# Negative parts, second norms and the masked key sums of a two-layer transformer block on one core

## The chip, the core and the metric

The kernel runs on one core of a Trainium2 chip. A core has a matrix engine (TensorE, "PE" in the profile, with its weight loads as "PEld"), three engines for everything else (VectorE "DVE", ScalarE "ACT", GpSimd "POOL"), and a queue that issues transfers ("SP"). Each runs its own instructions in program order and waits for the others on semaphores. The metric is device time in microseconds (us): the median of several runs.

## What is computed

Two transformer layers on 2 x 1024 rows of 256 numbers in float32. Only the parts that the change touches are shown in full: the norm, and the linear attention of the first layer with its elu.

```python
def _layernorm(x, axis=-1, eps=1e-05):
    m = jnp.mean(x, axis=axis, keepdims=True)
    v = jnp.var(x, axis=axis, keepdims=True)
    return (x - m) / jnp.sqrt(v + eps)

# layer 0 attention (16 heads of 16), on the normalised x
q = _heads(x @ q_w.T + q_b); k = _heads(x @ k_w.T + k_b); v = _heads(x @ v_w.T + v_b)
qp = jax.nn.elu(q) + 1.0
kp = jax.nn.elu(k) + 1.0
kv = jnp.einsum('bhsd,bhse->bhde', kp, v)
z = jnp.einsum('bhsd,bhd->bhs', qp, kp.sum(axis=2))[..., None]
attn = jnp.einsum('bhsd,bhde->bhse', qp, kv) / (z + EPS)
out = attn.transpose(0, 2, 1, 3).reshape(b, s, HID) @ o_w.T + o_b

# the whole
x = L0_attn_hidden_states                     # (2, 1024, 256), float32
xn = _layernorm(x)
x = x + _L0_attn_ref(xn, ...) + _L0_ffn_ref(xn, ...)   # ternary-weight SwiGLU, 256 -> 1024 -> 256
xn = _layernorm(x)
x = x + _L1_attn_ref(xn, ...) + _L1_ffn_ref(xn, ...)   # rotary softmax attention; SwiGLU with Hadamard transforms
return x
```

The kernel writes `elu(z) + 1` as `exp(min(z, 0)) + max(z, 0)`.

## The kernel before

**Tiling.** The 2048 rows are 16 tiles of 128 (`tt`), 4 chunks of 512 (`c`), and two halves (`b`) of 1024. One Python function, `work_order`, writes one list of pieces by hand, and every engine walks through this same list, taking the pieces that it has a part in. So the order on each engine is that of the list, and a piece that waits holds up all that its engine has behind it.

**First layer.** `main(0)` (the feed-forward: `gate`, `up`, `down` for 8 slices of each chunk) is woven with `side0` (the linear attention, then preparations of the second layer's weights) after a start-up of 12 side pieces. For a tile of keys, `kv_in` is: TensorE's product; VectorE adds the bias to keys `zk` (L1194) and to values `ve` (L1195); GpSimd takes `ek = min(zk, 0)` (L1565); ScalarE takes its exp (L1415); VectorE, in `kv_sum`, forms `max(zk, 0) + ek` (L1218). `kv_out` adds the product of keys and values up over 8 tiles in PSUM bank 2; a column of ones in `ve` gives the sum of the keys as a 129th column. After 8 tiles `kv_sums` multiplies by a block mask (a head sees its own 16 rows only): per 128 channels one multiplication by MASK (L1203) and one of eight mask columns by the key sum (L1204). `att_n` multiplies the queries by the result `kvb` (L840) and VectorE divides (L1224 to L1230).

For queries, `q0` is: VectorE takes `min(q + bias, 0)` (L1212) and `max(q + bias, 0)` (L1213) from PSUM, ScalarE the exp (L1419), GpSimd the sum (L1571).

**Norms.** `ln_stats` (VectorE statistics, a power on GpSimd, L1543), `ln_norm` (VectorE: four tiles `(x - mean) * rstd`, L1126, 128 x 256 each), `ln_turn` (TensorE transposes, L789; ScalarE copies the high part XH, L1401; VectorE the low part XL, L1132). Norms 0 to 3 are the first layer's, in the first 40 us; norms 4 to 7 are the second layer's and stand inside the woven list. GpSimd's `bias` (L1552) adds to X after the norm has read it.

The list around the points that matter, in its own order:

- first half's end: `kv_in 7`, `kv_sum 6`, `tern_cut`, `q0 1 0`, `bias 0`, `tern_abs 2` (ScalarE, L1410), `q0 1 1`, `kv_sum 7`, `kv_out 5, 6, 7`, `kv_sums 0`, `att_n 0`
- norm 4: `up 3`, `ln_norm 4`, `bias`, `gate 3`, `att_n 14`, `up 3`, `down 0`, `ln_turn 4`, `att_b`
- norm 5: `up 5`, `down 2`, `ln_norm 5`, `att_b`, `gate 6`, `prep_attn1` (ScalarE, 2.1 us of copies), `up 6`, `prep_down 0`, `down 3`, `ln_turn 5`, `gate 7`, `prep_down 1`

In a layer-0 slice ScalarE takes the tanh of the gate (`gate`, L1459) and a rounded copy of the product (`up`, L1467), VectorE the two products (L1250, L1259), GpSimd the remainder (L1604).

## Time and profile before

| | us |
|---|---|
| median of 3 runs (756.82 to 758.1) | 757.27 |
| the profiled execution's own time | 757.94 |
| its span, first to last instruction | 756.1 |
| busy: PE / DVE / ACT / POOL | 702.5 / 550.8 / 419.2 / 309.3 |
| PE busy, 0 to 80 us / 80 to 260 us | 53.1 / 164.9 |

A row of the timeline gives the start in us from the span's start, the duration, the engine, the line of the kernel, the operation and what it writes and reads; in brackets stand the idle time of the engine before it and what ended that. "x4" is four such instructions in a row, with the duration of all. Busy time of PE is not PE at its peak: the same matmul takes longer at the lower clock.

### The profile page before, as it was taken

To read this page: it belongs to the slowest core of one execution; us is meant where nothing else is said; L and a number is where in the kernel's file an instruction comes from. 1 tells how busy PE (TensorE), PEld (TensorE's weight loads), DVE (VectorE), ACT (ScalarE), POOL (GpSimd) and SP (SyncE) were. 2 spreads that over 40 slices of the span, in tenths; PEclk is the share of its full clock that TensorE was granted. 3 is DMA by queue.
4 is the path that set the end of the run, shared out by engine and by line. 5 is a ranking of instruction groups with operands and counts; after the bars stand their busy time and mean duration, and the time that the engine had idled before them with its cause. 6 is when DMAs were issued, how large, how long until landed. Compare 5 with 4: busy or idle time off the path is not lost.

```text
span 756.1 us, 10955 instructions
## 1 busy us (share of the span) xinstructions
PE 702.5 (93%) x4186; PEld 440.5 (58%) x4186; DVE 550.8 (73%) x896; ACT 419.2 (55%) x560; POOL 309.3 (41%) x285
## 2 busy tenths in 40 slices
PE   4778898979988989999999998999999999999998
PEld 3556797968666778777667675333333333333445
DVE  4896766676677846677888887888888188888415
ACT  2242223424534533343232435999999899999883
POOL 1248766344845856244343541121233213422510
PEclk9898999998999999999999998999999999999999
DMA  6127101001104372251301110344434244432221
GB/s 254 56 84 264 56 2 56 1 1 57 55 1 148 119 262 84 84 196 57 103 11 57 56 57 18 130 145 134 145 89 156 92 164 153 137 110 90 89 92 56
DMA packets 25847, 74.13 MB, mean 98 GB/s; under 512 B 4620, under 2 KB 5996, under 8 KB 24964
## 3 DMA queue, kind: packets, MB, share of 16 engines
q1 hardware_dynamic: 21268, 65.37, 25.9%
q0 software_dynamic: 3808, 7.60, 3.4%
q8 instruction: 33, 0.54, 0.3%
q10 hardware_dynamic: 720, 0.48, 0.2%
q14 instruction: 18, 0.15, 0.1%
HBM read 54.54 MB, written 23.06 MB: 103 GB/s over the span
## 4 chain that ended last, share of the span: by engine, by line
PE 60%; POOL 2%; DVE 2%; ACT 1%; issue 1%; DMA 0%; SPq 0%; DVEq 0%; POOLq 0%; ACTq 0%
PE PS L1020 17%; PE PS L758 12%; PE PS L1006 12%; PE PS L764 8%; PE PS L989 6%; PE PS L979 4%; DVE mx L1321 1%; POOL sg L1613 1%; ACT P L1505 1%; POOL rot L1633 1%; POOL rot L1634 1%; DMA scr_k<-spl 0%; PE PS L995 0%; POOL hl L1604 0%; ACT spl L1487 0%
## 5 line engine op out<-in xcount | busy, mean ns | idle before, releaser
L1505 ACT ACTIVATE P<-PS 128x1024 f32<-128x1024 f32 x256 | 249.4, 1025 | 31.6 <-PE PS L1006 31.2
L1328 DVE TENSOR_REDUCE mx<-PS 128x1 f32<-128x512 f32 x300 | 189.2, 683 | 34.5 <-PE PS L989 32.8
L1321 DVE TENSOR_REDUCE mx<-PS 128x2 f32<-128x1024 f32 x106 | 124.8, 1221 | 37.3 <-PE PS L979 37.0
L1020 PE MATMUL PS<-P,VV 128*32 128x512 f32 x1024 | 137.4, 608 | 0.1
L1604 POOL TENSOR_TENSOR hl<-sg,hh 128x512 fp32r<-128x512 f32 x64 | 84.4, 1319 | 120.0 <-ACT hh L1475 67.4
L1006 PEld LDWEIGHTS PS<-QS,KS 64*128 64x128 f32 x512 | 49.0, 185 | 124.0 <-ACT P L1505 110.8
L1006 PE MATMUL PS<-QS,KS 64*128 64x512 f32 x512 | 117.7, 459 | 2.2 <-DVE mx L1321 1.8
L989 PE MATMUL PS<-KM,QM 64*128 64x512 f32 x300 | 82.3, 402 | 0.0
L1461 ACT ACTIVATE sg<-PS,cols 128x512 f32<-128x512 f32 x32 | 22.1, 690 | 81.9 <-PE PS L758 81.9
L1613 POOL TENSOR_TENSOR sg<-sg,us 128x512 f32<-128x512 f32 x32 | 42.1, 1315 | 37.4 <-ACT us L1470 37.4
L758 PE MATMUL PS<-XH,UGH 128*128 128x512 f32 x128 | 54.1, 422 | 1.6 <-ACT sg L1461 0.8
L758 PE MATMUL PS<-XL,UGH 128*128 128x512 f32 x128 | 50.5, 394 | 0.0
L758 PE MATMUL PS<-XH,UGL 128*128 128x512 f32 x128 | 50.0, 390 | 0.0
L1467 ACT ACTIVATE hh<-sg 128x512 fp32r<-128x512 f32 x32 | 20.2, 632 | 53.5 <-DVE sg L1259 53.5
L1020 PEld LDWEIGHTS PS<-P,VV 128*32 128x32 f32 x1024 | 20.3, 108 | 40.1 <-issue 34.5
L989 PEld LDWEIGHTS PS<-KM,QM 64*128 64x128 f32 x300 | 38.8, 188 | 3.8 <-DVE mx L1328 0.7
L979 PE MATMUL PS<-KM,QM 64*128 64x512 f32 x212 | 39.9, 448 | 0.8 <-DVE mx L1321 0.6
L1459 ACT ACTIVATE sg<-PS,s 128x512 f32<-128x512 f32 x32 | 21.9, 684 | 32.2 <-PE PS L758 32.0
L764 PE MATMUL PS<-DH,hh 128*128 128x256 f32 x128 | 38.0, 297 | 0.0
L1250 DVE SCALAR_TENSOR_TENSOR sg<-sg,PS 128x512 f32<-128x512 f32 x32 | 21.9, 683 | 20.3 <-ACT sg L1459 20.2
L1470 ACT ACTIVATE us<-PS,cols 128x512 f32<-128x512 f32 x32 | 22.0, 688 | 25.5 <-PE PS L758 25.5
L764 PE MATMUL PS<-DL,hh 128*128 128x256 f32 x128 | 36.1, 282 | 0.0
(208 smaller groups left out, 1406.2 us busy)
## 6 DMA issues: line engine op xcount, KB each, us to landing
QM<-scr_q SPq DMA_DIRECT2D x16, 512.0 KB, 4.3
KM<-scr_k SPq DMA_DIRECT2D x16, 512.0 KB, 5.2
QS<-scr_q SPq DMA_DIRECT2D x16, 512.0 KB, 4.4
KS<-scr_k SPq DMA_DIRECT2D x16, 512.0 KB, 5.2
scr_q<-spl SPq DMA_DIRECT2D x24, 256.0 KB, 3.4
scr_k<-spl SPq DMA_DIRECT2D x24, 256.0 KB, 3.5
scr_o<-OE POOLq DMA_DIRECT2D x14, 256.0 KB, 2.7
stg<-in_tern SPq DMA_DIRECT2D x3, 1024.0 KB, 4.8
```

What stands on the lines that cost most here:

```text
L758: i = e.matmul(out, l, r, start=start and j == 0, stop=stop and j == len(pairs) - 1)
L764: i = e.matmul(out[:, r * 256:r * 256 + 256], l, x, start=first and r == 0 and j == 0, stop=last and j == len(pairs) - 1, skip_group_check ...
L979: e.matmul(bank[b + h], QM[p % 2][hr, qt * 128:(qt + 1) * 128], KM[p % 2][hr, chunk(half)], start=True, stop=True).then_inc(q["mt"], 1)
L989: e.matmul(bank[b], QM[p % 2][hr, qt * 128:(qt + 1) * 128], KM[p % 2][hr, chunk(half)], start=True, stop=True).then_inc(q["mt"], 1)
L1006: i = e.matmul(bank[b + h], KS[p % 2][hr, kt * 128:(kt + 1) * 128], QS[p % 2][hr, chunk(half)], start=True, stop=True)
L1020: i = e.matmul(PS[32 * c:32 * c + 32, 7, :], v_head(8 * b + kt, 2 * j + c // 2), P[s % 4][:, chunk(c // 2 + 2 * (c % 2))], start=(kt == 0) ...
L1321: e.tensor_reduce(mx[p % 2][:, :, qt, half], PS[:, b:b + 2, :], AX.X, ALU.max).then_inc(q["mx"], 2)
L1328: e.tensor_reduce(mx[p % 2][:, h, qt, half:half + 1], bank[b], AX.X, ALU.max).then_inc(q["mx"], 1)
L1461: e.activation(s[:, :], bank[b], ACT.Silu, scale=col("wsg", m)).then_inc(q["t"], 1)
L1505: e.activation(P[s % 4][:, half * 1024:(half + 1) * 1024], PS[:, b:b + 2, :].rearrange("p b n -> p (b n)"), ACT.Exp).then_inc(q["ex"], 1)
L1604: e.tensor_tensor(hl[f % 4][:, :], sg[f % 3][:, :], r32(hh[f % 4][:, :]), ALU.subtract).then_inc(q["hl"], 1)
L1613: e.tensor_tensor(s[:, :], s[:, :], us[f % 4][:, :], ALU.mult).then_inc(q["h"], 1)
```

## The change

- **Keys.** GpSimd's minimum (L1565) goes. ScalarE takes `ek = relu(-zk)` itself, then `exp(-ek)` as before in its place in the list.
- **Queries.** VectorE's minimum (L1212) goes. ScalarE takes `relu(-(q) - bias)` from PSUM (with a negated bias column made once), then `exp(-...)`. VectorE's maximum (L1213) now waits until ScalarE's relu has read the bank.
- **Norms 4 to 7.** VectorE only forms `-mean * rstd` (128 x 4, new tile `nmr`); ScalarE does the four tiles as `Identity(x * rstd + nmr)`. The waits for the buffers go with them.
- **Key sums.** `ve` has eight columns of ones instead of one, so the product has 136 columns instead of 129 per 128 channels; MASK is widened by its own eight columns; `kv_sums` is one multiplication of 128 x 272 instead of four instructions.

```diff
 SEMAPHORES = """
-init lns lnv lnd lnr lnn lnb lnh lnl bx fold w0h w0l sus
+init lns lnv lnd lnm lnr lnn lnb lnh lnl bx fold w0h w0l sus
 ta ts tc tl tp tt suh sgd
-kvp kvz kvv kvm kve kvk kvo kvs
+kvp kvz kvv kvm kve kvk kvo kvs mask
 qp qn qr qe qg
...
         IDN = sb("IDN", 25.5, [128, 128])
-        MASK = sb("MASK", 26, [128, 128])
+        MASK = sb("MASK", 26, [128, 136])
         ONES = sb("ONES", 27, [128, 128])
...
         mxc = [sb(f"mxc{i}", 27.8125 + i / 16, [128, 16]) for i in range(2)]
+        MINUS_QB = sb("MINUS_QB", 27.96875, [128, 2])
         MINUS_HALF = sb("MINUS_HALF", 27.9375, [128, 4])
...
         ek = [sb(f"ek{i}", 128 + i, [128, 256]) for i in range(4)]
-        ve = [sb(f"ve{i}", 132 + 1.25 * i, [128, 2, 129]) for i in range(4)]
-        kvb = [sb(f"kvb{i}", 137 + i * 0.5625, [128, 136]) for i in range(2)]
+        ve = [sb(f"ve{i}", 132 + 1.25 * i, [128, 2, 136]) for i in range(4)]
+        kvb = sb("kvb", 137, [128, 2, 136])
         zs = [sb(f"zs{i}", 139 + 2 * i, [128, 512]) for i in range(2)]
...
         mv = [sb(f"mv{i}", 207.5 + i / 32, [128, 4, 2]) for i in range(2)]
+        nmr = [sb(f"nmr{i}", 207.625 + i / 32, [128, 4]) for i in range(2)]
         rstd = [sb(f"rstd{i}", 207.5625 + i / 32, [128, 4]) for i in range(2)]
...
                 for g in range(2):
-                    o = e.matmul(bank[2][:, g * 129:(g + 1) * 129], zk[j][:, g * 128:(g + 1) * 128], ve[j][:, g, :],
+                    o = e.matmul(bank[2][:, g * 136:(g + 1) * 136], zk[j][:, g * 128:(g + 1) * 128], ve[j][:, g, :],
                                  start=(i == 0 and g == 0), stop=(i == 7), skip_group_check=True)
...
                 for g in range(2):
-                    i = e.matmul(bank[b][:, g * 136:(g + 1) * 136], QP[:, g, ts], kvb[g][:, :], start=True, stop=True)
+                    i = e.matmul(bank[b][:, g * 136:(g + 1) * 136], QP[:, g, ts], kvb[:, g, :], start=True, stop=True)
                 i.then_inc(q["an"], 1)
...
                 for i in range(4):
-                    e.memset(ve[i][:, :, 128:129], 1.0).then_inc(q["init"], 1)
+                    e.memset(ve[i][:, :, 128:136], 1.0).then_inc(q["init"], 1)
                 e.memset(MINUS_HALF[:, :], -0.5).then_inc(q["init"], 1)
...
                 e.wait_ge(q["lnr"], n + 1)
-                if n == 6:
-                    e.wait_ge(q["pu"], 4)
-                if n == 7:
-                    e.wait_ge(q["lnb"], 14)
+                if n >= 4:
+                    e.scalar_tensor_tensor(nmr[i][:, :], mv[i][:, :, 0], -1.0, rstd[i][:, :], ALU.mult, ALU.mult).then_inc(q["lnm"], 1)
+                    return
                 for t in range(4):
...
                 e.tensor_scalar(s16b[:, :], cols[:, z:z + 8], 1.0 / 32, None, ALU.mult).then_inc(q["sus"], 1)
+                e.tensor_scalar(MINUS_QB[:, :], cols[:, COLS["qb0"][0]:COLS["qb0"][0] + 2], -1.0, None, ALU.mult).then_inc(q["sus"], 1)
+                e.wait_ge(d["c"], 48)
+                e.tensor_scalar(MASK[:, 128:136], MASK[:, 0:128:16], 0.0, None, ALU.add).then_inc(q["mask"], 1)
...
                     e.wait_ge(q["an"], 8)
-                for g in range(2):
-                    e.tensor_tensor(kvb[g][:, 0:128], bank[2][:, g * 129:g * 129 + 128], MASK[:, :], ALU.mult)
-                    i = e.tensor_scalar(kvb[g][:, 128:136], MASK[:, 0:128:16], bank[2][:, g * 129 + 128:g * 129 + 129], None, ALU.mult)
-                i.then_inc(q["kvs"], 1)
+                e.wait_ge(q["mask"], 1)
+                e.tensor_tensor(kvb[:, :, :], bank[2][:, 0:272].rearrange("p (g n) -> p g n", g=2),
+                                MASK[:, :].rearrange("p (o n) -> p o n", o=1).broadcast_to([128, 2, 136]), ALU.mult).then_inc(q["kvs"], 1)
...
                 i = 2 * c + m
-                e.wait_ge(q["qp"], i + 1)
-                if i >= 2:
-                    e.wait_ge(q["qg"], i - 1)
-                e.tensor_scalar(zs[m][:, :], bank[b], col("qb0", m), 0.0, ALU.add, ALU.min).then_inc(q["qn"], 1)
+                e.wait_ge(q["qn"], i + 1)
                 e.tensor_scalar(QP[:, m, chunk(c)], bank[b], col("qb0", m), 0.0, ALU.add, ALU.max).then_inc(q["qr"], 1)
...
                 e.dma_start(IDN[:, :], ident_d).then_inc(d["idn"], 16)
-                for t, src in ((MASK, mask_d), (HAD, had_d), (BKV, bkv_d)):
+                for t, src in ((MASK[:, 0:128], mask_d), (HAD[:, :], had_d), (BKV[:, :], bkv_d)):
                     e.dma_start(t[:, :], src).then_inc(d["c"], 16)
+
+            def ln_norm(n):
+                c, i = n % 4, n % 2
+                if n < 4:
+                    return
+                e.wait_ge(q["lnm"], n - 3)
+                if n == 6:
+                    e.wait_ge(q["pu"], 4)
+                if n == 7:
+                    e.wait_ge(q["lnb"], 14)
+                for t in range(4):
+                    e.activation(ln_buffer(n)[:, t, :], X[:, 4 * c + t, :], ACT.Identity, bias=nmr[i][:, t:t + 1], scale=rstd[i][:, t:t + 1]).then_inc(q["lnn"], 1)
...
             def kv_in(tt, b):
+
                 j = tt % 4
+                e.wait_ge(q["kvz"], tt + 1)
+                if tt >= 4:
+                    e.wait_ge(q["kvk"], tt - 3)
+                e.activation(ek[j][:, :], zk[j][:, :], ACT.Relu, scale=-1.0).then_inc(q["kvm"], 1)
                 e.wait_ge(q["kvm"], tt + 1)
-                e.activation(ek[j][:, :], ek[j][:, :], ACT.Exp).then_inc(q["kve"], 1)
+                e.activation(ek[j][:, :], ek[j][:, :], ACT.Exp, scale=-1.0).then_inc(q["kve"], 1)
             def q0(c, m, b):
-                e.wait_ge(q["qn"], 2 * c + m + 1)
-                e.activation(zs[m][:, :], zs[m][:, :], ACT.Exp).then_inc(q["qe"], 1)
+
+                i = 2 * c + m
+                e.wait_ge(q["qp"], i + 1)
+                if i == 0:
+                    e.wait_ge(q["sus"], 3)
+                if i >= 2:
+                    e.wait_ge(q["qg"], i - 1)
+                e.activation(zs[m][:, :], bank[b], ACT.Relu, bias=MINUS_QB[:, m:m + 1], scale=-1.0).then_inc(q["qn"], 1)
+                e.wait_ge(q["qn"], i + 1)
+                e.activation(zs[m][:, :], zs[m][:, :], ACT.Exp, scale=-1.0).then_inc(q["qe"], 1)
...
                 e.tensor_tensor(raw, raw, over_tiles(WSD, 8), ALU.mult).then_inc(q["fold"], 1)
-
-            def kv_in(tt, b):
-                j = tt % 4
-                e.wait_ge(q["kvz"], tt + 1)
-                if tt >= 4:
-                    e.wait_ge(q["kvk"], tt - 3)
-                e.tensor_scalar(ek[j][:, :], zk[j][:, :], 0.0, None, ALU.min).then_inc(q["kvm"], 1)
```

(the lists `parts` of ScalarE and GpSimd are changed to fit)

## Rows read from the trace of the kernel before

**Rows 1.** Stages of 20 us: us, busy (x instructions) of PE, PEld, DVE, ACT, POOL; PEclk; DMA
```profile
100.00:120.00 20.00, 20.00 (x127) 18.01 (x126) 13.66 (x28) 5.98 (x11) 13.44 (x10) 1.00 0.01 2
120.00:140.00 20.00, 17.64 (x105) 14.84 (x104) 13.16 (x27) 6.86 (x12) 9.13 (x8) 1.00 0.15 53
160.00:180.00 20.00, 14.68 (x75) 12.45 (x74) 13.03 (x33) 6.27 (x11) 7.65 (x6) 0.83 0.10 27
```
**Rows 2.** Waits of PE, 0 to 200 us: us in total, times, longest
```profile
PE PS L823 <- DVE zk L1218: 4.4, 2, 2.2
PE PS L840 <- DVE at L1230: 3.0, 1, 3.0
```
**Rows 3.** Timeline, ScalarE, 20 to 62 us: start, us, what [idle before <- releaser]
```profile
36.99 0.42 ACT L1415 ACTIVATE ek<-ek 128x256 f32<-128x256 f32 x1 [3.27 <-POOL ek L1565]
55.03 1.89 ACT L1410 ACTIVATE TD<-stg 128x2048 fp32r<-128x2048 f32 x1
```
**Rows 4.** Timeline, VectorE, 20 to 62 us: norms, products and keys of the first half
```profile
40.32 0.75 DVE L1212 TENSOR_SCALAR zs<-PS,cols 128x512 f32<-128x512 f32 x1
47.16 0.43 DVE L1218 SCALAR_TENSOR_TENSOR zk<-zk,ek 128x256 f32<-128x256 f32 x1 [0.41 <-ACT ek L1415]
56.36 0.47 DVE L1218 SCALAR_TENSOR_TENSOR zk<-zk,ek 128x256 f32<-128x256 f32 x1
57.88 0.29 DVE L1203 TENSOR_TENSOR kvb<-PS,MASK 128x128 f32<-128x128 f32 x1 [1.04 <-PE PS L823]
58.08 0.98 DVE L1204 TENSOR_SCALAR kvb<-MASK,PS 128x8 f32<-128x8 f32 x1
59.18 1.10 DVE L1204 TENSOR_SCALAR kvb<-MASK,PS 128x8 f32<-128x8 f32 x1
```
**Rows 5.** Timeline, TensorE, 55 us on: the first attention matmul
```profile
60.39 1.24 PE L840 MATMUL PS<-kvb,QP 128*128 128x136 f32 x4 [2.55 <-issue]
```
**Rows 6.** Timeline, GpSimd, 55 us on: a bias addition
```profile
56.50 2.54 POOL L1552 TENSOR_TENSOR X<-X,OB 128x1024 f32<-128x1024 f32 x1
```
**Rows 7.** Groups of one shape, 0 to 200 us: busy, mean ns of one | idle before
```profile
L1230 DVE TENSOR_TENSOR at<-PS,rz 128x256 f32<-128x256 f32 x16 | 6.8, 425 | 1.4
L823 PE MATMUL PS<-ve,zk 128*128 128x129 f32 x64 | 10.0, 284 | 4.4 <-DVE zk L1218 4.4
L1459 ACT ACTIVATE sg<-PS,s 128x512 f32<-128x512 f32 x25 | 17.1, 684 | 25.0 <-PE PS L758 24.8
L1426 ACT ACTIVATE AH<-PS 128x512 fp32r<-128x512 f32 x8 | 4.7, 586 | 0.0
```
**Rows 8.** Timeline, VectorE, around the first second-layer norm
```profile
164.96 2.33 DVE L1126 TENSOR_SCALAR XD<-X,mv,rstd 128x256 f32<-128x256 f32 x4
167.21 0.68 DVE L1250 SCALAR_TENSOR_TENSOR sg<-sg,PS 128x512 f32<-128x512 f32 x1
168.36 0.42 DVE L1230 TENSOR_TENSOR at<-PS,rz 128x256 f32<-128x256 f32 x1
```
**Rows 9.** Timeline, ScalarE, the same place
```profile
165.62 0.67 ACT L1459 ACTIVATE sg<-PS,s 128x512 f32<-128x512 f32 x1
```
**Rows 10.** Timeline, TensorE, the same place
```profile
168.89 1.06 PE L789 MATMUL PS<-IDN,XD 128*128 128x128 f32 x8 [2.84 <-issue]
```
**Rows 11.** Timeline, ScalarE, at the second of these norms
```profile
184.41 0.69 ACT L1459 ACTIVATE sg<-PS,s 128x512 f32<-128x512 f32 x1 [0.81 <-PE PS L758]
187.77 0.83 ACT L1441 ACTIVATE DH<-PS,s16b 128x256 fp32r<-128x256 f32 x2
```
**Rows 12.** Timeline, TensorE, after that norm
```profile
189.56 1.12 PE L876 MATMUL PS<-stg,HAD 128*128 128x512 f32 x2 [0.67 <-DVE DL L1278]
```
**Rows 13.** Timeline, TensorE, around the third and the fourth
```profile
228.90 0.50 PE L758 MATMUL PS<-XH,W1H 128*128 128x512 f32 x1 [1.42 <-DVE XL L1132]
235.84 0.50 PE L758 MATMUL PS<-XH,TG 128*128 128x512 f32 x1 [1.57 <-DVE sg L1250]
260.74 0.44 PE L789 MATMUL PS<-IDN,XD 128*128 128x128 f32 x2 [0.83 <-DVE XD L1126]
275.73 0.55 PE L758 MATMUL PS<-W1H,XH 128*128 128x256 f32 x1 [2.10 <-ACT VV L1493]
```

More of the change, by code:

```diff
@@ L1527, in last @@
                     e.activation(LH[:, qs], OE[0][:, qs], ACT.Copy).then_inc(q["lh"], 1)
-            parts = {f.__name__: f for f in (start, ln_turn, w0h, tern_abs, kv_in, q0, att_t, prep_attn1, prep_down, prep_ug, gate, up,
+            parts = {f.__name__: f for f in (start, ln_norm, ln_turn, w0h, tern_abs, kv_in, q0, att_t, prep_attn1, prep_down, prep_ug, gate, up,
                                              hidden, qk_split, v, max_rows, scores, out, load_exp, last)}
@@ L1674, in low @@
                     e.wait_ge(q["fill"], 2)
-            parts = {f.__name__: f for f in (ln_stats, bias, fold, kv_in, q0, butterfly, low_attn1, difference, total, up, hidden, ones_v, qk_join, load_wl, out, recip, times, high, low)}
+            parts = {f.__name__: f for f in (ln_stats, bias, fold, q0, butterfly, low_attn1, difference, total, up, hidden, ones_v, qk_join, load_wl, out, recip, times, high, low)}
             for name, *args in order:
```

## The prediction

> **What bounds the kernel now.** I read the stages of 20 us first. From 80 us on TensorE is nearly always busy: between 100 and 120 us it works all 20.00 us at full clock while VectorE has 6.3 us to spare [rows 1]. So work taken from VectorE, ScalarE or GpSimd is worth nothing there by itself; only a place where TensorE stands still, and what ends that stand, can give or take time. The list of TensorE's waits in the first 200 us is short [rows 2]: the last key sum of each half (4.4 us in two places, the longest 2.2), one wait of 3.0 us for the divided tile `at`, and two waits whose releaser the view calls "issue". The timelines show what these are: 2.55 us before the first `att_n` at 60.39 us [rows 5], in which VectorE works off `kv_sums` [rows 4], and 2.84 us before the transposes of norm 4 at 168.89 us [rows 10], which need a bank that `att_n 14` frees when VectorE's L1230 of 168.36 us is done [rows 8]. Later there are waits of 0.67 us [rows 12] and of 1.42, 1.57, 0.83 and 2.10 us [rows 13]. The reader is to ask of each: which engine's queue does its releaser stand in, and does the change shorten or lengthen that queue?
>
> **Keys and queries up to 60 us.** Before 60 us TensorE is starved and VectorE's queue sets the pace. Three things get shorter. (1) ScalarE's exp of 36.99 us came only after 3.27 us of waiting for GpSimd's minimum, and the copy XH, on which VectorE waits, stood behind it [rows 3]; with relu and exp back to back on ScalarE I place XH 0.7 us earlier. (2) Two minima of 0.75 us [rows 4], overlapped a little, leave VectorE's queue ahead of the next two key tiles: 1.3 us. The maxima's new wait costs nothing here, since ScalarE has nothing between XH and these relus. (3) VectorE's wait of 0.41 us for an exp at 47.16 us [rows 4] goes, and some contention with GpSimd around it; I take 0.7 in all. So `q0 1 0` comes 2.7 us earlier. What is late next: ScalarE has the 1.89 us of `tern_abs 2` [rows 3] between the two q0. Placed by the same durations, relu and exp of `q0 1 0` end at 51.3 us, the Abs at 53.2, the relu of `q0 1 1` at 53.9, and VectorE, which now waits for it with `kv_sum 7` queued behind, ends its maximum at 54.7. `kv_sum 7` starts at 54.6 instead of 56.36 us [rows 4]: 1.8 us earlier, though two more minima are gone. And there GpSimd's bias addition of 2.54 us, which follows its sum of `q0 1 0` [rows 6], lies over it, from about 53.1 to 55.6. The rows show what that does: L1204, which reads MASK from SBUF for 8 columns, started at 58.08 and lasted 0.98 us, to 59.06; the addition had started at 56.50 and ended at 59.04 [rows 4, 6]. L1203, 128 columns out of PSUM, took 0.29 us in the same time. So an operation with both operands in SBUF may wait for GpSimd's to end, and `kv_sum 7` has both there. I take an end at 55.9 instead of 56.83: 0.9 us, with 1.8 as the other end.
>
> **Key sums.** Four instructions from 57.88 to 59.18 + 1.10 = 60.28 us, 2.40 us [rows 4], wholly on the path, since TensorE starts at 60.39 [rows 5]. The one that replaces them reads 272 columns from PSUM; L1230 takes 0.425 us for 256 [rows 7], so 0.44. It saves 1.96 us. In the second half TensorE has `gate 4` between, and I count nothing. The seven extra columns of the products: between nothing and 7/129 of 10.0 us [rows 7] = 0.5; I take 0.2, as their time is mostly fixed cost. Sum at 60 us: -0.9 - 1.96 = -2.9 us (to -3.8).
>
> **Does it carry on?** From 60 to 81 us the chain runs through VectorE's ternary steps and the 3.0 us wait [rows 2], with nothing of the change in it; all queues, GpSimd's biases too, move by about the same. GpSimd's missing minima (16) and VectorE's missing ones lie beside a full TensorE. At the second half's end `q0 2 1` puts its relu behind ScalarE's hh copy, so VectorE loses there about what it gained by `q0 2 0`: 0 (-0.4 to +0.3) on the other 2.2 us wait.
>
> **Norms 4 to 7.** VectorE loses four instructions (2.33 us) [rows 8] and gets one of 128 x 4. ScalarE gets four of 128 x 256 with two per-partition operands. Their price: a pair with one such operand lasts 0.83 us [rows 11], so 1.66 for four; a second operand costs 0.684 - 0.586 = 0.10 each [rows 7], so 2.06; I take 2.1, with 1.66 and 4 x 0.684 = 2.7 as ends. The Trainium skill ("ScalarE: Activation LUTs", What ACT_TABLE_LOAD costs) gives 186 ns plus 0.833 per element plus 93 per pointer operand with 93 ns of overlap: an estimate of 2.06 us by that page, and the sum would be the same.
>
> The point is what stands behind them on ScalarE. At norm 4 that is the tanh of `gate 3` at 165.62 us [rows 9]: it moves to 167.7 and ends at 168.4. VectorE's L1250 wants it at 167.21 [rows 8], so L1250 starts at 168.45 although VectorE is free long before, `att_n 14`'s division stands behind L1250, and TensorE gets its bank at 170.1 instead of 168.89 [rows 8, 10]: +1.25 us (0.8 to 1.8). hh, XH and XL of this norm follow with the same shift. At norm 5 the next tanh had 0.81 us of slack [rows 11]; it moves by 2.1 - 0.8 = 1.3, the 2.1 us of `prep_attn1` behind it too, a small wait behind these takes 0.3, and DH at 187.77 [rows 11] comes 1.0 later. TensorE waited for what follows DH already, 0.67 us at 189.56 [rows 12]: +1.0 (0.6 to 1.6). At norm 6 the wait at 228.90 us grows by 1.1, but 7 us later TensorE waits 1.57 us for a VectorE chain [rows 13] that is held by GpSimd's bias addition meanwhile and hardly moves: +0.2 (0 to 1.1). At norm 7 TensorE's 0.83 us for XD goes, but the 2.10 us wait at 275.73 [rows 13] hangs on a chain over GpSimd, ScalarE and a transfer that the norm isn't part of: -0.2 (-0.8 to 0).
>
> The same page's Rules for kernel authors send relu, max and min to VectorE, not ScalarE, which speaks against this change. For float32 out of PSUM the rows do not bear it out: VectorE's minimum takes 0.75 us [rows 4], ScalarE's one-operand activation of the shape 0.684 [rows 7]. The page also says that relu and identity are in every table set, so no table load is added; no trace of before shows either function.
>
> **The sum.** -2.9 + 0.2 + 0 + 1.25 + 1.0 + 0.2 - 0.2 = -0.45 us. Against the profiled execution's 757.94 us (span 756.1 and 1.8 around it) that is 757.5. This execution lies 0.67 above the median of 757.27, so the median to expect is 756.8. I take 0.2% (1.5 us) as what a measurement of this kernel can tell from no change.
>
> **Rivals.** *Faster:* GpSimd's addition doesn't cover `kv_sum 7`, and the norms cost their lower ends. -3.8 + 0.2 + 0.8 + 0.6 - 0.2 = -2.4: 754.9 us. For it speaks that a shift of half a microsecond decides the cover; against it that both must hold. Chance 0.27. *Slower, by the clock:* between 160 and 180 us, around norm 4, the granted clock was 0.83 against 1.00 in the full stage [rows 1]; 0.17 x 20 = 3.4 us of full-speed time, around a stand of 2.84 us. The stands at norms 5 and 6 grow from 0.67 and 1.42 to about 1.7 and 2.5 us. If TensorE falls to the lower of its two levels (1.2 GHz of 2.4) there as well, each costs about half of that, 1.7 us; the point is whether a stand of about 2.5 us is enough. With one and a half of them 756.8 + 2.5 = 759.3 us. Against it: the second 2.2 us stand, at 131 us, lies in a stage at clock 1.00 [rows 1]. Chance 0.2. *The gain doesn't carry:* something between 60 and 165 us holds its own time, and only the norms' cost is left with half of the gain: 756.8 + 1.4 = 758.2. I saw no such wait. Chance 0.1. The forecast has 0.43.
>
> **How the numbers follow.** The forecast and the third case lie mostly within 0.2% of 757.27 (755.8 to 758.8); the forecast's own range is 755.2 to 758.4. Faster 0.30, the same 0.49, slower 0.21. The range, 754.2 to 759.6, reaches to both outer rivals.
>
> **What would show it.** The first `att_n` at 57.4 us instead of 60.39 (56.6 if nothing covers `kv_sum 7`). L1203's successor at 0.44 us. The four Identity at 2.1 us with a tanh right behind, a stand of TensorE before norm 4's transposes of about 4.1 us, and 1.7 us before `prep_down 1`. PEclk of 180 to 240 us tells of the clock. The prediction fails if ScalarE's four cost over 2.7 us, if the lead at 60 us isn't found at 160 us, or if table loads appear.

## The result, and the profile after

The changed kernel takes 752.65 us (median of 5 runs, 750.98 to 754.84), before 757.27: ratio 0.994, 95% interval 0.992 to 0.996. Measured again beside the last experiments it took 751.09 us against 757.42, ratio 0.992 (0.990 to 0.994). The forecast of 756.8 and the range of 754.2 to 759.6 were both too high: the change gains 4.6 us where 0.5 had been expected. The profiled execution took 753.33 us, its span is 751.2 us.

Section 1 of the page after: busy time of the engines.

```profile
PE 700.9 (93%) x4186; PEld 441.4 (59%) x4186; DVE 532.0 (71%) x872; ACT 438.4 (58%) x600; POOL 293.8 (39%) x269
```

Timeline of TensorE after: the places that answer to [rows 5], the second long wait of [rows 2], [rows 10], [rows 12] and [rows 13].

```profile
57.93 1.25 PE L842 MATMUL PS<-kvb,QP 128*128 128x136 f32 x4 [0.58 <-issue]
...
126.12 0.70 PE L825 MATMUL PS<-ve,zk 128*128 128x136 f32 x4 [0.59 <-DVE zk L1218]
...
165.01 1.94 PE L791 MATMUL PS<-IDN,XD 128*128 128x128 f32 x8 [3.92 <-DVE at L1230]
...
186.31 1.12 PE L878 MATMUL PS<-stg,HAD 128*128 128x512 f32 x2 [1.43 <-DVE DL L1278]
...
226.49 0.50 PE L760 MATMUL PS<-XH,W1H 128*128 128x512 f32 x1 [2.13 <-DVE XL L1133]
...
232.38 0.50 PE L760 MATMUL PS<-XH,TG 128*128 128x512 f32 x1 [0.52 <-DVE sg L1250]
...
272.17 0.39 PE L760 MATMUL PS<-W1H,XH 128*128 128x256 f32 x1 [2.08 <-ACT VV L1518]
```

A start in this list less its counterpart before is the lead that the kernel has at that point. It was 2.46 us at the first attention product (60.39 before), and 4.77 us at the last key product of the second half, which began at 130.89 us before, after a wait of 2.23 us. That wait is now 0.59 us. The norms take back part of the lead: 3.88 us before norm 4's transposes, 3.25 at 186.31. At 272.17 us it is 3.56 and stays within 0.1 us of that up to 460 us, where TensorE's clock adds to it (last section).

The stages that answer to [rows 1]: us, busy of PE, PEld, DVE, ACT, POOL; PEclk.

```profile
100.00:120.00 20.00, 20.00 (x127) 18.04 (x126) 13.77 (x28) 7.95 (x15) 9.23 (x6) 1.00 0.11 29
120.00:140.00 20.00, 19.41 (x122) 17.30 (x121) 11.47 (x25) 8.93 (x14) 8.97 (x8) 1.00 0.06 25
```

TensorE is full between 100 and 120 us in both kernels. What happened in that stage shows only in the next one, where its busy time rises from 17.64 us [rows 1] to 19.41.

**Where the missed 2.2 us came from.** The timeline of the kernel before around the end of the second half, all engines (start, us, what [idle before <- releaser]):

```profile
117.38 2.40 POOL L1580 TENSOR_TENSOR stg<-stg 128x1024 f32<-128x1024 f32 x1
...
119.74 1.47 POOL L1604 TENSOR_TENSOR hl<-sg,hh 128x512 fp32r<-128x512 f32 x1
121.19 0.84 POOL L1565 TENSOR_SCALAR ek<-zk 128x256 f32<-128x256 f32 x1
122.06 0.42 ACT L1415 ACTIVATE ek<-ek 128x256 f32<-128x256 f32 x1 [2.86 <-POOL ek L1565]
122.38 0.68 ACT L1459 ACTIVATE sg<-PS,s 128x512 f32<-128x512 f32 x1
123.09 0.69 DVE L1250 SCALAR_TENSOR_TENSOR sg<-sg,PS 128x512 f32<-128x512 f32 x1 [3.03 <-ACT sg L1459]
...
129.69 1.06 DVE L1218 SCALAR_TENSOR_TENSOR zk<-zk,ek 128x256 f32<-128x256 f32 x1
```

And the changed kernel at the same pieces of work:

```profile
116.27 0.40 ACT L1430 ACTIVATE ek<-zk 128x256 f32<-128x256 f32 x1
...
116.70 0.42 ACT L1432 ACTIVATE ek<-ek 128x256 f32<-128x256 f32 x1
...
117.02 0.67 ACT L1484 ACTIVATE sg<-PS,s 128x512 f32<-128x512 f32 x1
...
117.72 0.69 DVE L1250 SCALAR_TENSOR_TENSOR sg<-sg,PS 128x512 f32<-128x512 f32 x1 [0.49 <-ACT sg L1484]
...
125.56 0.41 DVE L1218 SCALAR_TENSOR_TENSOR zk<-zk,ek 128x256 f32<-128x256 f32 x1
```

Before, the keys of tile 15 lay ready at 118.9 us, but GpSimd reached their minimum only at 121.19, behind a butterfly step and a `hl`. ScalarE's exp waited for it, the tanh of the next gate stood behind the exp, VectorE waited 3.03 us for the tanh, and all that VectorE had to do ahead of the last key sum moved with it. After, relu and exp stand back to back, and VectorE waits 0.49 us. The lead at VectorE's L1250 is 5.37 us. TensorE had enough other work until 128.7 us, so nothing of this is seen in its row before the last key product.

### The profile page after: what moved, and what is told of

Same layout as the page of the kernel before. It is cut to its first block, busy times and chain, and to the rows that moved or that the text cites. A ratio compares the mean times of both kernels' runs of the same rounds, so it can differ in the third digit from the quotient of the medians.

```text
span 751.2 us, 10957 instructions
## 1 busy us (share of the span) xinstructions
PE 700.9 (93%) x4186; PEld 441.4 (59%) x4186; DVE 532.0 (71%) x872; ACT 438.4 (58%) x600; POOL 293.8 (39%) x269
## 4 chain that ended last, share of the span: by engine, by line
PE 60%; POOL 2%; DVE 2%; ACT 1%; issue 1%; DMA 1%; SPq 0%; DVEq 0%; POOLq 0%; ACTq 0%
PE PS L1022 17%; PE PS L760 12%; PE PS L1008 12%; PE PS L766 8%; PE PS L991 6%; PE PS L981 5%; DVE mx L1321 1%; POOL sg L1631 1%; ACT P L1530 1%; DMA scr_k<-spl 1%; POOL rot L1651 1%; POOL rot L1652 0%; PE PS L997 0%; ACT spl L1512 0%; ACT us L1495 0%
## 5 line engine op out<-in xcount | busy, mean ns | idle before, releaser
L1250 DVE SCALAR_TENSOR_TENSOR sg<-sg,PS 128x512 f32<-128x512 f32 x32 | 21.9, 684 | 24.5 <-ACT sg L1484 24.5
```

## The experiments

Three sets of runs, each set on one chip beside runs of the kernel before (medians 757.0, 757.09 and 757.42 us). Ratios are to those. A fourth set of single profiled executions comes at the end.

| kernel | median us | ratio (95% interval) |
|---|---|---|
| norms_back | 749.88 | 0.991 (0.989 to 0.993) |
| keys_back | 755.93 | 0.998 (0.997 to 0.999) |
| norm_late | 751.61 | 0.993 (0.991 to 0.994) |
| min15_first | 754.45 | 0.9975 (0.996 to 0.999) |
| mix | 749.89 | 0.991 (0.989 to 0.993) |
| sums_only | 757.23 | 1.000 (0.998 to 1.001) |
| queries_back | 751.54 | 0.993 (0.991 to 0.995) |
| keys_only | 752.95 | 0.994 (0.9925 to 0.996) |
| keys_sums | 750.9 | 0.993 (0.991 to 0.995) |
| best | 747.6 | 0.988 (0.986 to 0.990) |
| sums_min8 | 754.73 | 0.997 (0.996 to 0.999) |
| the change, again | 751.09 | 0.992 (0.990 to 0.994) |

The starts of TensorE at six points of each kernel's profiled execution, read from its timeline as above: A first attention product, B the one after the long wait of [rows 2], C last key product of the second half, D transposes of norm 4, E the work that waits for DL [rows 12], F the wait for VV [rows 13]; then the span.

| kernel | A | B | C | D | E | F | span |
|---|---|---|---|---|---|---|---|
| before | 60.39 | 80.87 | 130.89 | 168.89 | 189.56 | 275.73 | 756.1 |
| before_2 | 60.60 | 81.60 | 131.57 | 169.56 | 189.43 | 273.98 | 751.8 |
| the change | 57.93 | 78.27 | 126.12 | 165.01 | 186.31 | 272.17 | 751.2 |
| the change, again | 57.34 | 77.46 | 125.31 | 164.19 | 185.53 | 271.32 | 750.4 |
| norms_back | 57.15 | 77.27 | 125.11 | 162.91 | 183.58 | 269.46 | 749.5 |
| norms_back_2 | 56.97 | 77.08 | 124.88 | 162.67 | 183.37 | 269.77 | 747.3 |
| norm_late | 56.78 | 76.90 | 124.73 | 161.66 | 183.95 | 268.38 | 748.5 |
| mix | 56.86 | 77.11 | 124.77 | 161.68 | 182.67 | 268.38 | 745.9 |
| queries_back | 56.67 | 77.62 | 126.71 | 165.58 | 187.28 | 271.88 | 749.5 |
| keys_sums | 56.57 | 77.50 | 126.56 | 164.37 | 185.01 | 271.09 | 751.2 |
| keys_sums_2 | 56.53 | 77.47 | 123.68 | 161.48 | 182.45 | 267.01 | 747.3 |
| best | 56.65 | 77.61 | 123.82 | 160.74 | 181.70 | 267.33 | 745.1 |
| best_2 | 56.65 | 77.57 | 125.38 | 162.30 | 182.95 | 268.87 | 749.2 |
| keys_only | 58.65 | 79.53 | 127.18 | 165.16 | 185.81 | 271.97 | 752.1 |
| min15_first | 60.32 | 80.79 | 128.62 | 166.59 | 187.56 | 272.01 | 752.4 |
| keys_back | 59.46 | 80.28 | 129.74 | 168.63 | 189.98 | 276.06 | 753.5 |
| sums_min8 | 59.14 | 80.36 | 130.42 | 169.80 | 189.96 | 274.63 | 754.6 |
| sums_only | 58.78 | 81.49 | 131.63 | 171.03 | 191.69 | 277.89 | 758.2 |

Kernels with the same instructions up to a point differ there by up to 1.2 us at A and 1.4 at C for the change and its norm variants, and by 2.9 us at C between two profiles of `keys_sums` itself. Stretches at TensorE's lower clock make up much of that; the last section tells of them. The distance from C to D is steadier: 38.00 and 37.99 us in the two profiles of before, 37.80 and 37.79 in those of `norms_back`, 38.89 and 38.88 in those of the change, 36.92 in both of `best`.

**norms_back**: the norms on VectorE again.

```diff
 def ln_norm(n):
-    if n >= 4:
-        e.scalar_tensor_tensor(nmr[i][:, :], mv[i][:, :, 0], -1.0, rstd[i][:, :], ALU.mult, ALU.mult).then_inc(q["lnm"], 1)
-        return
+    if n == 6:
+        e.wait_ge(q["pu"], 4)
+    if n == 7:
+        e.wait_ge(q["lnb"], 14)
```

> The changed kernel with norms 4 to 7 back on VectorE, all else kept. Theory (the norms on ScalarE are a loss that the rest of the change outweighs): the transposes of norm 4 start about 1.1 us earlier than in the changed kernel (at about 163.9 us), the stand before prep_down 1 falls back to about 0.7 us, and the whole takes about 1.5 us less, 751.2 us. Rival (relieving VectorE of the norms is where the gain comes from): about 2 us more than the changed kernel, 754.5 us or above.

Measured 749.88 us. From C to D it takes 37.80 us, the change 38.89: norm 4 costs 1.09 us on ScalarE. From C to E it is 58.47 against 60.19: the two norms 1.72. The second profiles of both kernels give the same distances within 0.03 us. The part of the change that was to relieve VectorE costs time. This rests on the marks; the intervals of the medians overlap (749.88 us here, 752.65 and 751.09 the change).

**norm_late**: ScalarE's part of each norm is taken after the tanh that follows it in the list.

```diff
+            held = None
             for name, *args in order:
+                if name == "ln_norm" and args[0] >= 4:
+                    held = args
+                    continue
                 if name in parts:
                     parts[name](*args)
+                    if held is not None and name == "gate":
+                        ln_norm(*held)
+                        held = None
```

> The changed kernel with ScalarE's four Identity of norms 4 to 7 one piece later in its list, behind the tanh of the next gate. Theory (the loss at norm 4 is the tanh standing behind the norm): the transposes of norm 4 start at about 163.3 us instead of 165.0, norm 5 gains nothing since prep_attn1 and DH still stand behind it; 751.5 us. Rival (the loss is the later end of the norm itself): no change at norm 4 or a later start, 752.7 us or above.

Measured 751.61 us. The timeline of the change at norm 4:

```profile
160.65 2.06 ACT L1408 ACTIVATE XD<-X,nmr,rstd 128x256 f32<-128x256 f32 x4
...
162.62 0.67 ACT L1484 ACTIVATE sg<-PS,s 128x512 f32<-128x512 f32 x1
...
163.32 0.69 DVE L1250 SCALAR_TENSOR_TENSOR sg<-sg,PS 128x512 f32<-128x512 f32 x1 [3.17 <-ACT sg L1484]
```

and of `norm_late`:

```profile
159.26 0.67 ACT L1484 ACTIVATE sg<-PS,s 128x512 f32<-128x512 f32 x1
...
159.83 2.06 ACT L1408 ACTIVATE XD<-X,nmr,rstd 128x256 f32<-128x256 f32 x4
159.97 0.69 DVE L1250 SCALAR_TENSOR_TENSOR sg<-sg,PS 128x512 f32<-128x512 f32 x1 [1.21 <-ACT sg L1484]
```

The four instructions cost the same 2.06 us in both. With the tanh ahead of them C to D is 36.93 us, 1.96 under the change and 0.87 under VectorE's own norm. At norm 4 the price lay in what stood behind the instructions, not in the instructions. At norm 5 the same edit is worse: D to E takes 22.29 us instead of 21.30. There the change's four instructions (179.57 us, the tanh at 181.54) had run in part while ScalarE would have waited for the gate; now they follow a tanh of 177.19 (0.84 us of waiting for TensorE before it) at 177.78 us, and the weight copies, DH and the rest start behind all of them.

**mix**: norm 5 on VectorE, norms 4, 6 and 7 on ScalarE after the tanh.

```diff
-                if n >= 4:
+                if n >= 4 and n != 5:
                     e.scalar_tensor_tensor(nmr[i][:, :], mv[i][:, :, 0], -1.0, rstd[i][:, :], ALU.mult, ALU.mult).then_inc(q["lnm"], 1)
...
-                if n < 4:
+                if n < 4 or n == 5:
                     return
-                e.wait_ge(q["lnm"], n - 3)
+                e.wait_ge(q["lnm"], {4: 1, 6: 2, 7: 3}[n])
```

(with the edit of `norm_late`)

> The changed kernel with norm 5 back on VectorE, and with ScalarE's part of norms 4, 6 and 7 put behind the tanh of the gate that follows in the list. If the price of a norm on ScalarE is the wait of VectorE's product for the tanh behind it, both forms that avoid this wait add up: norms_back (749.9) less 1.25 at norm 4 (stand of 2.0 instead of 2.8 us) and less 1.4 at norm 6 (the 1.4 us wait gone) gives 747.2; from norm_late (751.6, though in its profile the last 75 us ran at the lower clock) less 1.5 to 1.9 at norm 5 gives 749.7. I expect 747.2 to 749.7, most likely 748.3; TensorE's transposes of norm 4 start near 161.7 and the first prep_down work that waits for DL near 182.3 (idle under 0.8). Rival: the gains of norm 4 and norm 5 are one and the same, given back at the next wait (for DL); then it is norms_back's 749.9 again, with the DL wait 0.8 us longer than there.

Measured 749.89 us, that of `norms_back`: by the medians the rival is right. By the marks C to E is 57.90 us, 0.57 under `norms_back`, and C to F 143.61 against 144.35. Against `norm_late`, which has F at the same 268.38 us, the 1.3 us won at E are gone at the third norm, where both wait 2.04 us for VectorE's product at 228.56 us. A gain of 0.7 us is left that these runs don't resolve. The expectation gives the last 75 us of `norm_late`'s profile a lower clock; the trace has a granted clock of 1.00 from 670 to 748 us, so that allowance had nothing under it.

**keys_back**: the change, with the keys' minimum on GpSimd.

```diff
 # ScalarE, kv_in
-                e.activation(ek[j][:, :], zk[j][:, :], ACT.Relu, scale=-1.0).then_inc(q["kvm"], 1)
                 e.wait_ge(q["kvm"], tt + 1)
-                e.activation(ek[j][:, :], ek[j][:, :], ACT.Exp, scale=-1.0).then_inc(q["kve"], 1)
+                e.activation(ek[j][:, :], ek[j][:, :], ACT.Exp).then_inc(q["kve"], 1)
 # GpSimd
+                e.tensor_scalar(ek[j][:, :], zk[j][:, :], 0.0, None, ALU.min).then_inc(q["kvm"], 1)
```

> The changed kernel with the keys' negative part back on GpSimd as a minimum, exp on ScalarE. Theory (the minimum in GpSimd's queue held back ScalarE's exp and, behind it, the tanh): the stand of TensorE near 126 us grows from 0.6 to over 2 us, and the lead there falls by 2 us, that at 60 us by about 0.5; 755.3 us. Rival (what moved the stand near 126 us is the queries' minimum taken from VectorE): the stand stays under 1 us and the time within 1 us of the changed kernel's 752.7.

Measured 755.93 us: 3.3 us above the first measurement of the change and 4.8 above the second. Its wait before C is 1.99 us again, with GpSimd's minimum at 120.64 us behind the same two instructions.

**min15_first**: the kernel before, in which GpSimd takes one minimum, that of tile 15, two instructions earlier.

```diff
+            mine = list(order)
+            mine.remove(("kv_in", 15, 0))
+            mine.insert(mine.index(("butterfly", 5)), ("kv_in", 15, 0))
-            for name, *args in order:
+            for name, *args in mine:
```

> The kernel before, with one change in GpSimd's own order: the keys' minimum of tile 15 ahead of butterfly 5 and of the hl in between. Theory (in the kernel before, this minimum stood behind 2.4 us of butterfly and 1.3 us of hl, and the exp and the tanh of ScalarE waited for it): the tanh at 122.4 us comes 2 us earlier, the stand of 2.2 us before the last kv_out at 130.9 us shrinks to about 0.5, and the kernel takes 1.7 us less than before, 755.5 us. Rival (the stand is set by VectorE's q0 work just before it): the stand stays at 2 us, 757.3 us.

Measured 754.45 us, 2.55 us under the kernel before in the same set. B is as before (80.79), C comes 2.27 us earlier after a wait of 0.57 us. So the place of this one instruction in GpSimd's queue held more than 2 us of the whole kernel's time.

**keys_only**: the kernel before with the keys' part of the change and nothing else (the edit of `keys_back` the other way round).

> The kernel before with nothing but the keys' part: ScalarE takes relu and exp of the keys, GpSimd has no minimum any more. If GpSimd's minimum in the queue behind butterfly and high part is what holds the end of the second half, the wait of 2.2 us at 131 us falls to about 0.6 although VectorE's other work is all still there; before 60 us the keys' exps come earlier: first attention matmul at 59.5 (58.9 to 60.1), at the second half's end 127.8, end 757.0 - 0.9 - 2.0 = 754.0. Rival: it needs the queries' part too (VectorE's minima of 0.75 us keep the place late): wait there 1.5 or more, end 755.5 or above.

Measured 752.95 us, 4.1 us under before, where the whole change gained 4.6 and 6.3 us in its two measurements. A is 1.74 us earlier than before, C 3.71, after a wait of 0.56 us. VectorE's minima of the queries are all still there, so they were not what held the end of the second half.

**sums_only**: the kernel before with the key sums' part of the change (its hunks for `ve`, `kvb`, MASK and `kv_sums`) and nothing else.

> The kernel before with nothing but the key sums of the change: 136 columns instead of 129 and one masked multiplication of 128 x 272 instead of four instructions; minima and norms as before. By the step of the prediction: the multiplication starts at 57.9 as before, takes 0.44 us, the first attention matmul starts at 58.45 instead of 60.39, nothing more at 131 us (wait there 2.2 us as before, start 128.95), and the rest moves as a whole: 757.0 - 1.9 = 755.1. Rival 1: the columns cost 0.5 us in all and more of it lies on the path: 755.6. Rival 2: something between 60 and 131 us (GpSimd's minimum for the last keys) holds its own time: then the wait at 131 us grows by 1.9 and the end is at 756.8.

Measured 757.23 us: no gain that twelve runs (752.22 to 760.0 us) can show. The profiled execution is the longest of the twelve. The lead of 1.6 us at A is there, and at B it has become a lag of 0.6 us. The timeline between them:

```profile
65.77 3.20 DVE L1159 TENSOR_SCALAR TD<-stg,s 128x2048 fp32r<-128x2048 f32 x1
67.85 2.26 POOL L1605 TENSOR_TENSOR hl<-sg,hh 128x512 fp32r<-128x512 f32 x1
...
70.08 0.84 POOL L1566 TENSOR_SCALAR ek<-zk 128x256 f32<-128x256 f32 x1
...
70.95 0.42 ACT L1416 ACTIVATE ek<-ek 128x256 f32<-128x256 f32 x1 [6.92 <-POOL ek L1566]
71.28 0.61 ACT L1468 ACTIVATE hh<-sg 128x512 fp32r<-128x512 f32 x1
71.79 0.58 ACT L1427 ACTIVATE AH<-PS 128x512 fp32r<-128x512 f32 x1
...
72.40 0.69 DVE L1238 TENSOR_TENSOR AL<-PS,AH 128x512 fp32r<-128x512 f32 x1 [2.84 <-ACT AH L1427]
73.15 0.84 PE L840 MATMUL PS<-kvb,QP 128*128 128x136 f32 x4 [2.33 <-DVE AL L1238]
```

GpSimd works through three bias additions of 2.4 us and a `hl` before it comes to the minimum of tile 8, at 70.08 us; ScalarE stands for 6.92 us in front of the exp (3.43 us in the kernel before), with hh and AH behind it, and TensorE gets a wait of 2.33 us that the kernel before didn't have. VectorE's ternary step had moved earlier onto GpSimd's addition and took 3.20 us instead of 1.36. The theory expected here was wrong and the second rival right in kind, only that the place is at 70 us and not at 131, where the wait is 2.20 us as before.

**sums_min8**: `sums_only`, with GpSimd's minimum of tile 8 ahead of the last bias addition.

```diff
+            mine = list(order)
+            late = [p for p in mine if p[:2] == ("kv_in", 8)][0]
+            at = mine.index(late)
+            mine.remove(late)
+            while mine[at][0] != "bias":
+                at -= 1
+            mine.insert(at, late)
-            for name, *args in order:
+            for name, *args in mine:
```

> sums_only with one instruction moved in GpSimd's own order: the minimum for tile 8 stands one bias addition and one hl earlier (near 65.5 us instead of 70.1). If that minimum's place is what swallowed the sums' lead, the new wait of 2.3 us for AL at 73.15 us is gone, the attention matmul after the long wait comes near 79.3 instead of 81.5, the one at 131.6 us near 129.3, and the end is 1.9 us under sums_only's: 755.2. Rival: VectorE's own ternary step of 3.2 us (1.36 in the kernel before) that now ran beside GpSimd's bias additions swallowed it; then the wait for AL stays over 1.5 us, and the end is at 757.

```profile
66.59 0.85 POOL L1566 TENSOR_SCALAR ek<-zk 128x256 f32<-128x256 f32 x1 [0.74 <-DVE zk L1196]
...
67.47 0.42 ACT L1416 ACTIVATE ek<-ek 128x256 f32<-128x256 f32 x1 [2.09 <-POOL ek L1566]
...
70.28 0.69 DVE L1238 TENSOR_TENSOR AL<-PS,AH 128x512 fp32r<-128x512 f32 x1 [1.18 <-ACT AH L1427]
```

Measured 754.73 us. That is 2.5 under `sums_only`, though the two come from different sets and their intervals overlap. The wait for AL is gone and B is at 80.36 instead of 81.49, half of what was expected (79.3). A later ternary step on VectorE, at 70.89 us, took 2.21 us beside GpSimd's `hl`, where it had taken 1.30; whether that held the rest back is not shown. The first ternary step on VectorE takes 1.33 us again, so the two causes named in the expectation ended together; that the minimum's place set off both is shown, what each is worth by itself is not.

**queries_back**: the change, with the queries' minimum on VectorE.

```diff
 # VectorE, q0
-                e.wait_ge(q["qn"], i + 1)
+                e.wait_ge(q["qp"], i + 1)
+                if i >= 2:
+                    e.wait_ge(q["qg"], i - 1)
+                e.tensor_scalar(zs[m][:, :], bank[b], col("qb0", m), 0.0, ALU.add, ALU.min).then_inc(q["qn"], 1)
```

(and ScalarE only the exp, as before)

> The changed kernel with the queries' minimum back on VectorE (exp with scale 1 on ScalarE, as before), keys, sums and norms as changed. Theory: VectorE gets 0.75 us back twice ahead of the last key tiles of the first half, so kv_sum 7 comes about 1 us later, first attention matmul at 58.9 instead of 57.9; but VectorE no longer waits 2.28 us for ScalarE's relu, so the loss may be smaller. After 80 us the queries' minima cost nothing of themselves except the one of q0 2 1 just ahead of the last key sum at 125 us, where VectorE waited 1.28 us for ScalarE: 0 to 0.7 earlier there. End 753.2 (752.4 to 753.9). Rival: moving the queries is what frees the second half's end as well; then the wait there is 2 us again and the end is at 755.

Measured 751.54 us, no different from the change (751.09 and 752.65). A does not come later, as had been expected, but 0.1 to 1.3 us earlier than in the six profiles of the four kernels that are the change up to there. Taking 0.75 us twice from VectorE brought nothing, for the reason that the 60 us rows show below.

**keys_sums** and **best**: keys and key sums alone; and the same with the norms as in `mix`.

> The kernel before with two parts of the change: the keys' relu and exp on ScalarE, and the key sums in one multiplication with 136 columns. Queries' minima and all norms stay on VectorE. Theory now held: GpSimd's minima of the keys hold the stage at 70 us as well (sums_only: the lead of 1.6 us at 58.78 us was gone at 81.49, because GpSimd reached the minimum of tile 8 only at 70.08, behind biases and a hl, and ScalarE's exp stood 6.9 us waiting with hh and AH behind it). With the minima gone, the sums' lead carries: first attention matmul at 56.7 (keys_only 58.65, less 1.95), the one after the 2.85 us wait at 77.6, last key product of the second half at 125.3, transposes of norm 4 at 163.3 with a stand of 2.84; end 753.0 - 1.9 = 751.1 from the keys_only median, or 749.9 + 1.2 at most from norms_back, whose queries go over ScalarE: with the queries' share of about 1 us taken back, 748.9. I expect 748.9 to 751.1. Rival: the sums are worth nothing with the keys moved either; then the mark at 77.6 is at 79.5 and the end at 753.

> keys_sums, and norms 4, 6 and 7 on ScalarE behind the next tanh (norm 5 on VectorE). If the three norms are worth what the stands say (2.0 instead of 2.8 us at norm 4, the 1.4 us wait of norm 6 against 0.5 more at the next): 0.7 to 0.9 us under keys_sums at the mark of 272 us and in the end. Rival: as between mix and norms_back, the medians do not differ (within 0.5 us) since the clock after the waits varies by more from one execution to the next.

Measured 750.9 and 747.6 us. The first is within its expectation and shows what `sums_only` could not: beside the keys' part the sums' lead lasts (B at 77.50, `keys_only` 79.53). Its C came 1.3 us later than expected, after a stretch of lower clock (last section). Between 750.9 and 752.95 the intervals overlap, so the gain of about 2 us rests on the marks. `best` is 9.8 us under the kernel before, the fastest median of all, and 3.3 under `keys_sums`. Only 0.9 us of that is in the waits (C to D 36.92 against 37.81); much of the rest is C's 2.74 us, from the lower clock at 80 us. From C to F nothing of the 0.9 us stands out: 143.51 and 143.49 us in the two profiles of `best`, 144.53 and 143.33 in those of `keys_sums`. A sixth execution (`best_2`) took 751.34 us, above all five of the first, so the 3.3 us are not to be relied on.

**after_again**: the change as it is.

> The changed kernel as it is, on the same chip as the others, for a ledger in which all parts are compared within one set: 752.65 was its median over 5 runs. Keys and sums without queries and norms (keys_sums) should lie 2 to 3.5 us under it: 2.8 from the norms (norms_back), and -0.3 to 1 from the queries (queries_back). Rival: the gains found separately overlap, and it is 751 or less.

Measured 751.09 us, so the costs found one by one don't add up to a distance from `keys_sums` (750.9). Of the 2.8 us given there for the norms the marks bear out 1.1 at D and 1.7 at E.

**before_2, norms_back_2, keys_sums_2, best_2**: four kernels once more, unchanged, one profiled execution each, for the clock after 430 us.

> The kernel before, unchanged, for a second profile. The granted clock of 430 to 520 us was 0.96 in all seven profiles of kernels whose norms 4 to 7 are on VectorE, this one among them, and 0.98 in six of the seven with norms on ScalarE. If the edit of the norms sets it, it is 0.96 here again; if it is chance, 0.98 is as likely. The waits of 3.0 us at 80.9 and of 2.2 us at 130.9 us are there again in any case, within 0.1 us.

> norms_back unchanged, second profile: the change with its norms on VectorE. By the norms' theory the clock of 430 to 520 us is 0.96 again, by chance either. From the last key product of the second half to norm 4's transposes 37.8 us, as in the first.

> keys_sums unchanged, second profile. By the norms' theory the clock of 430 to 520 us is 0.96, by chance either. The clock of 80 to 84 us was 0.54 in its first profile and 1.00 in best, with the same instructions so far; if that is chance it may be 1.00 here, and then the last key product of the second half comes near 124 instead of 126.56.

> best unchanged, second profile. By the norms' theory the clock of 430 to 520 us is 0.98, by chance either. If its median of 747.6 has a cause in the kernel up to 130 us, the clock of 80 to 84 us is 1.00 again and the last key product at 123.8; nothing in its instructions up to there differs from keys_sums, so I expect it anywhere between 123.8 and 126.7.

Measured 753.6, 749.25, 749.37 and 751.34 us. The granted clock of 430 to 520 us was 0.98, 0.98, 0.96 and 0.96: three of the four against the theory that the norms set it. The theory falls, chance stays. The kernel before took 757.94 us in its first profile and 753.6 in this one, with the same waits (2.95 us at B, 2.23 and 2.24 at C).

## Why the prediction was wrong, step by step

The terms of the sum beside the marks of the two profiled executions (lead gained is negative; the two norms are parted at the transposes of `at`, 178.61 us before and 174.51 after):

| term | predicted | measured |
|---|---|---|
| lead at 60 us | -2.9 | -2.46 |
| 60 to 81 us | 0 | -0.14 |
| second half's end | 0 | -2.17 |
| 131 to 162 us | 0 | -0.20 |
| norm 4 | +1.25 | +0.87 |
| norm 5 | +1.0 | +0.85 |
| norms 6 and 7 | 0 | -0.31 |
| more columns | +0.2 | in the rows above |
| 272 us to the end, above all the clock at 460 us | - | -1.34 |
| around the span | - | +0.29 |
| sum | -0.45 | -4.61 |

**The failed step** is the sentence "GpSimd's missing minima (16) and VectorE's missing ones lie beside a full TensorE", with the 0 set for the second half's end. It holds for VectorE's minima (`queries_back`) and not for GpSimd's: `min15_first` shows 2.3 us for the place of one. `keys_only` shows 3.71 us at C for all of them, of which 1.74 are there at A already and 1.97 come after, and `keys_back` brings the wait before C back to 1.99 us. The rows for it were in the trace. [rows 2] gave a wait of 2.2 us with the name of VectorE's L1218, and I asked what stood in VectorE's queue ahead of it, the pieces of `q0 2 1`, and stopped there. VectorE itself had waited 3.03 us for ScalarE 6.6 us earlier, and ScalarE 2.86 us for GpSimd. A busy TensorE says that no wait has reached it yet; it does not say that none is on the way. The list of later waits also left out 1.36 us at 171.31 and 2.58 us at 213.98; the change hardly moved them (1.20 and 2.58 us after).

**Does it carry on?** Predicted that the lead at 60 us lasts, with "nothing of the change in it". Right as to time, wrong as to the reason. `sums_only` shows that in the kernel before such a lead is lost within 20 us to GpSimd's minimum of tile 8; it lasts in the changed kernel because this minimum is gone. The rival "the gain doesn't carry" named no place and got 0.1; the place existed.

**The lead at 60 us** was sized well: 2.46 us in this execution, 3.05 to 3.61 in the five other profiles of kernels that are equal to the change up to there, 2.9 predicted. Half a microsecond of the difference is clock: the four key products before A, after a wait of 3.38 us, took 1.25 us in this execution (granted clock 0.50) and 0.70 us in the other five. The rows of the change:

```profile
53.33 2.35 POOL L1577 TENSOR_TENSOR X<-X,OB 128x1024 f32<-128x1024 f32 x1
...
54.30 0.75 DVE L1213 TENSOR_SCALAR QP<-PS,cols 128x512 f32<-128x512 f32 x1 [2.28 <-ACT zs L1442]
54.97 0.99 DVE L1218 SCALAR_TENSOR_TENSOR zk<-zk,ek 128x256 f32<-128x256 f32 x1
...
57.39 0.44 DVE L1207 TENSOR_TENSOR kvb<-PS,MASK 128x272 f32<-128x272 f32 x1 [1.43 <-PE PS L825]
```

The new wait for ScalarE's relu (2.28 us), GpSimd's addition over `kv_sum 7` (0.99 us, ended at 55.96; 55.9 predicted) and the masked product (0.44 us, as predicted) are all there. The shares inside were off: the keys alone give 1.74 us at A, where 1.4 were counted, and the queries take away 0.1 to 0.7 us at the last four key products (55.39 us in `queries_back`, 55.50 to 56.11 us in the six profiles with them), where 0.5 was placed.

Of that cover the page "SBUF — State Buffer" of the Trainium skill (SBUF: two separate sides) says that a GpSimd operation and a VectorE operation with two SBUF inputs exclude each other for a whole instruction. The trace agrees: `kv_sum 7`, an operation that takes 0.41 us elsewhere, started inside the addition and ended 0.28 us after it did (55.68 us).

**The norms.** ScalarE's four at 2.06 us, tanh right behind, stand of 3.92 us before the transposes (4.1 predicted), 1.43 us at `prep_down 1` (1.7 predicted): the mechanism and the sizes hold. Net, norm 4 costs 0.87 us and not the 1.09 of its start, since the clock came back earlier after it: the granted clock was 0.50 from 170 to 175 us before, and in the change 0.50 from 166 to 169 and 1.00 again from 172 us. No table load was added: three before, three after.

**More columns.** The group of key products and the two new functions of ScalarE, one shape each, 0 to 200 us: busy, mean ns of one | idle before.

```profile
L825 PE MATMUL PS<-ve,zk 128*128 128x136 f32 x64 | 10.9, 302 | 4.0 <-DVE zk L1218 4.0
...
L1430 ACT ACTIVATE ek<-zk 128x256 f32<-128x256 f32 x16 | 6.6, 415 | 23.0 <-DVE zk L1198 22.9
...
L1442 ACT ACTIVATE zs<-PS,MINUS_QB 128x512 f32<-128x512 f32 x8 | 5.5, 682 | 2.9 <-PE PS L760 2.8
```

The products took 0.9 us more in all than in [rows 7], more than the 0.2 to 0.5 of the forecast. Most of that is not the columns: between 100 and 120 us, at a granted clock of 1.00 in both kernels, a product's mean is 273 ns before and 278 after, which makes 0.3 us for 64.

**The rivals.** *Faster*, at 754.9 us, came nearest by luck, with 2 us too little: neither of its conditions held, since the addition did cover `kv_sum 7` and the norms did not cost their lower ends. *Slower, by the clock* did not come: the stands of 1.43 and 2.13 us left the granted clock between 180 and 260 us as it was. The size of the clock's play, though, was left out of the range altogether, and it alone moved this profile by 1.34 us. The two profiles of the kernel before differ by 4.3 us, and two executions of it on one chip (753.6 and 757.65 us) by 4.1, about as much as the change brings; that the change is faster rests on its five and six runs, not on one pair of profiles.

## What to carry to other kernels

When a wait names its releaser, walk on: look at what that engine waited for, back until an engine is found that had no idle time in that stretch; the cause is the queue that it works off. A light instruction in the queue of a slow engine, between two engines that pass work to each other, costs its place in the queue and not its duration (0.84 us of work held 2.2 us), so try to reorder it or move it to the engine that uses its result next. And when work goes to an engine for relief, put it behind the instruction that others wait for: at norm 4 the same 2.06 us cost 1.1 us ahead of the tanh and gained 0.9 behind it. Look at each place by itself, though: at norm 5, where DH, for which TensorE waits, stands behind both, the same move cost 1.0 us.
